# Four experts and a channel attention joined in one block, three quarters normalised ahead, TensorE's fillers and the value matrix moved

## The chip, the cores and the metric

One core of one Trainium2 chip runs the whole program in one launch. The metric is the device time of one execution in microseconds (us). Engines are named as in the profile: PE (TensorE matmul), PEld (its weight loads), DVE (VectorE), ACT (ScalarE), POOL (GpSimd), SP (SyncE).

## The reference, cut to what matters

A tower of four layers on 4 x 512 tokens of width 64, in float32. The residual stream is `h`; every half layer is `h = h + f(layernorm(h))`. The change touches the second half of L1, all of L2, and the way into L3:

```python
h = h + _L1_attn_ref(_layernorm(h, axis=-1), ...)    # softmax attention, one head
h = h + _L1_ffn_ref(_layernorm(h, axis=-1), ...)     # graph scores, then 4 experts, top 2
h = h + _L2_attn_ref(_layernorm(h, axis=-1), ...)    # channel attention
h = h + _L2_ffn_ref(_layernorm(h, axis=-1), ...)     # 8 experts, top 2
h = h + _L3_attn_ref(_layernorm(h, axis=-1), ...)    # softmax attention, 8 heads
h = h + _L3_ffn_ref(_layernorm(h, axis=-1), ...)     # causal attention, then 8 experts
# channel attention, per batch and per head of 4 channels:
k, v = layernorm(k), layernorm(v)                    # over groups of 4 channels, ddof 1, gain, offset
kv = einsum('bhnd,bhne->bhde', k, v) / HW
out = einsum('bhnd,bhde->bhne', q, kv)
return gelu((out + x) @ W_proj.T + b_proj) + x
```

## The kernel before, in words

The 2048 tokens are 16 tiles of 128. A quarter q (0 to 3) is the 4 tiles of one batch, 512 tokens. `H` holds the residual stream, `X` the normalised input, both tokens by channels; `XT2` is `X` turned, channels by tokens. PSUM has 8 banks, `PS[:, bank]`. Each engine's order is written out by hand and held together by semaphores; a `Block` ends with a barrier of all engines.

**experts** (line 1432; 4 experts in L1, 8 in L2, there as 4 pairs) walks over 16 units (quarter, expert): PE `up` (L1473), ACT the activation (L1542), PE `gates` (L1484) spreads the gate weights, DVE multiplies (L1570), PE `down` (L1504). At a quarter's end ACT copies one output bank (L1548), DVE adds the other (L1576), PE turns the sum back (`turn`, L1511), and DVE adds it to `H` in two steps (L1561, L1563). With an `Entering` object in `after`, the next stage's layernorm of quarters 0 to 2 runs meanwhile: DVE `sums` (L2240, L2242), POOL `centre` (L2250, L2253), DVE `root` (L2259, L2261), POOL `apply` (L2268, L2271). A quarter's `sums` and the previous one's `root` stand in DVE's order between its other work. With `keeps_turn`, the turn of the last quarter is left to the next stage as `before["last_turn"]`.

**L1's experts** (`l1_ffn`, L3208) have none of this: the block ends, and **l2_attn** (L3271) opens a block whose `entry` normalises all four quarters on DVE and ACT (L2342 to L2352), turns them on PE (L2533) and copies them on ACT (L2510), while POOL prepares the weights (`kv_weights`, 18 small chained steps, L3249) and then adds `X` to `H` for all tiles in one instruction (L3421).

**The channel attention** projects keys and values (`kv`, L3300) and queries (L3306) and the skip path (`skip`, L3315). Each quarter goes through five DVE steps, in `schedule`, skewed by two: step 0 adds the bias out of PSUM (L3441), ACT squares (L3393), step 1 sums (L3445), ACT roots (L3398), step 2 adds epsilon (L3448), step 3 is the reciprocal (L3451), step 4 the product (L3454). I write (k,q) for step k of quarter q. Gain and offset are two POOL instructions per quarter (L3425, L3427), for the last quarter two DVE instructions (L3477, L3480). Then per quarter: PE `met` (L3322), DVE `masked_` (L3458), PE `mixing` (L3331), ACT copies (L3402), PE `heads` (L3341), DVE adds the bias (`biased`, L3464), ACT applies gelu (L3406), POOL adds to `H` (L3430), DVE for the last one (L3468).

**unread** (L3346, L368, L851) and **dense** (L2546) are matmuls whose result nobody reads; they only fill TensorE's time.

**l2_ffn** (L3491) has its `entry`, the experts with `after`, and in the same block **l3_attn**, which is `linked_attentions` (L643). At its start PE turns the value matrix (L754) and quarter 0 (L2293), does the kept turn, projects (L765), and runs the 8 row products `rows` (L775), whose maxima DVE takes (L1000); DVE splits them in five steps (`split`, L1011 to L1019), PE turns them (`maxima`, L797), and the columns and exponentials follow (L807, L816, L941). The value matrix `VO` is cleared, given its ones and filled by DVE at this stage's start (L976, L978, L983); row products wait for it because it frees a bank. Eight `unread` stand ahead of `maxima(0)`.

**l1_attn** is `softmax_attention` (L189), with 4 `unread` ahead of its row products (L303), 2 after each of the four, and 6 later; POOL meanwhile normalises the last quarter twice (L2250 to L2280), and that quarter's turn (L2293) stands ahead of `maxima(0)` (L317).

## Time and profile before

| what | us |
|---|---|
| runs, median of 3 | 918.92 (918.06 to 924.89) |
| the profiled execution, its own time | 922.85 |
| its span, first to last instruction | 921.0 |
| PE busy | 808.4 (88%) |
| DVE busy | 644.0 (70%) |
| ACT busy | 370.6 (40%) |
| POOL busy | 231.7 (25%) |
| mean granted clock of PE | 0.947 |

The times in all rows are us from the span's start. The clock is a share of full speed: 1.00 is 2.4 GHz, 0.50 is 1.2 GHz. DMA plays no part in the stages at issue.

### The profile page before, as it was taken

Reading aid. Unit: us, or ns where it says so; the run is one execution under the profiler, and the core shown is the slowest. Engines: PE = TensorE matmul, PEld = TensorE weight load, DVE = VectorE, ACT = ScalarE, POOL = GpSimd, SP = SyncE. Lnnn points to the kernel's source line nnn. Section 1 sums busy time; section 2 is a strip of 40 time slices with the busy share of each in tenths; the row PEclk is TensorE's granted clock in tenths of the full one; section 3 lists DMA queues with packets and bytes.
Section 4 is the critical chain, followed back from the end, with each engine's and each line's share of the span. In section 5 each row is a group of like instructions: output and inputs, shape, how many; then the busy total and the mean of one; then the engine's idle time right before and its main releaser. Section 6 shows DMA issues by size and latency. Waiting matters only on the chain. (4 is left out here: it accounts for less than half of the span.)

```text
span 921.0 us, 19874 instructions
## 1 busy us (share of the span) xinstructions
PE 808.4 (88%) x8099; PEld 432.8 (47%) x8099; DVE 644.0 (70%) x1724; ACT 370.6 (40%) x642; POOL 231.7 (25%) x292
## 2 busy tenths in 40 slices
PE   0896879979999887998788979999999999978997
PEld 0566757755544345774365433333333334434443
DVE  3988548877896468998775874656566456757665
ACT  0213354444663342323544614555554333344443
POOL 1900003223546213440150131113132424210000
PEclk9898989998999999999986978999999998997999
DMA  8500030000000001000000000000000000000000
GB/s 284 159 1 2 1 96 3 3 2 2 1 1 2 1 2 49 1 2 1 1 2 1 1 1 1 1 1 1 2 1 2 1 1 1 2 1 1 7 7 13
DMA packets 11494, 15.28 MB, mean 17 GB/s; under 512 B 8390, under 2 KB 9446, under 8 KB 10406
## 3 DMA queue, kind: packets, MB, share of 16 engines
q1 hardware_dynamic: 9984, 12.91, 4.5%
q10 hardware_dynamic: 1418, 1.09, 0.5%
q8 instruction: 65, 1.06, 0.5%
q14 instruction: 27, 0.22, 0.1%
HBM read 13.47 MB, written 0.52 MB: 15 GB/s over the span
## 5 line engine op out<-in xcount | busy, mean ns | idle before, releaser
L1000 DVE TENSOR_REDUCE mx<-PS 128x2 f32<-128x1024 f32 (+3 forms) x96 | 102.4, 1088 | 71.1 <-PE PS L775 59.4
L941 ACT ACTIVATE arena<-PS 128x1024 f32<-128x1024 f32 (+3 forms) x96 | 85.8, 917 | 122.2 <-PE PS L816 109.0
L807 PE MATMUL PS<-arena 32*128 32x512 f32 (+3 forms) x384 | 90.8, 611 | 7.4 <-ACT arena L927 2.7
L775 PE MATMUL PS<-arena 32*128 32x512 f32 (+3 forms) x384 | 90.6, 640 | 4.4 <-DVE arena L983 3.8
L832 PE MATMUL PS<-arena 128*64 128x512 f32 (+3 forms) x384 | 92.3, 565 | 0.4 <-DVE arena L1059 0.4
L1542 ACT ACTIVATE arena<-PS,f_b_sb 128x512 f32<-128x512 f32 x96 | 61.2, 684 | 38.5 <-PE PS L1473 35.0
L1570 DVE TENSOR_TENSOR arena<-arena,PS 128x512 f32<-128x512 f32 x96 | 61.6, 683 | 15.5 <-PE PS L1484 15.5
L1473 PE MATMUL PS<-XT,late 64*64 64x512 f32 x384 | 61.5, 606 | 2.9 <-issue 1.5
L1504 PE MATMUL PS<-arena,late 64*64 64x512 f32 x384 | 58.1, 596 | 0.0
L1104 POOL TENSOR_TENSOR H<-H,arena 128x256 f32<-128x256 f32 x32 | 23.5, 736 | 116.9 <-DVE arena L1034 114.5
L807 PEld LDWEIGHTS PS<-arena 32*128 32x128 f32 x384 | 27.6, 189 | 53.0 <-issue 32.2
L1754 DVE TENSOR_TENSOR arena<-arena,PS 106x512 f32<-106x512 f32 (+1 forms) x48 | 30.8, 684 | 20.9 <-PE PS L1654 13.7
L2546 PE MATMUL PS<-identh 128*128 128x512 bf16 x91 | 29.5, 464 | 16.8 <-PEq L1197 4.0
L2072 PE MATMUL PS<-late 128*128 128x128 fp8e5 x512 | 35.6, 235 | 8.3 <-DVE late L1981 8.3
L832 PEld LDWEIGHTS PS<-arena 128*64 128x64 f32 x384 | 19.9, 136 | 46.7 <-issue 39.9
L1722 ACT ACTIVATE arena<-PS 106x512 f32<-106x512 f32 (+1 forms) x48 | 26.0, 594 | 39.2 <-PE PS L1642 39.2
L775 PEld LDWEIGHTS PS<-arena 32*128 32x128 f32 x384 | 28.3, 198 | 25.4 <-issue 14.9
L2072 PEld LDWEIGHTS PS<-late 128*128 128x128 fp8e5 x512 | 32.9, 106 | 13.0 <-DVE late L1981 11.0
L3047 POOL TENSOR_TENSOR arena<-NB,vals 128x1280 f32<-128x1280 bf16 x11 | 25.7, 2339 | 35.2 <-DVE vals L3122 35.2
L1395 POOL TENSOR_TENSOR H<-H,arena 128x256 f32<-128x256 f32 x28 | 20.4, 730 | 53.0 <-DVE arena L1358 50.9
L1059 DVE SCALAR_TENSOR_TENSOR arena<-arena,Cc 128x256 f32<-128x256 f32 x32 | 15.6, 498 | 25.4 <-ACT arena L941 25.2
L1642 PE MATMUL PS<-XT,late 64*64 64x512 f32 (+1 forms) x192 | 30.8, 612 | 1.0 <-DVE L L2368 1.0
(480 smaller groups left out, 1724.0 us busy)
## 6 DMA issues: line engine op xcount, KB each, us to landing
arena<-in_rel SPq DMA_DIRECT2D x4, 1024.0 KB, 11.8
late<-in_edges SPq DMA_DIRECT2D x2, 1024.0 KB, 11.7
arena<-in_adj SPq DMA_DIRECT2D x1, 1024.0 KB, 6.6
late<-in_w_f_w SPq DMA_DIRECT2D x2, 512.0 KB, 3.9
Cc<-in_consts SPq DMA_DIRECT2D x1, 916.0 KB
arena<-in_ids ACTq DMA_DIRECT2D x1, 800.0 KB
late<-in_w_f_w SPq DMA_DIRECT2D x2, 340.0 KB, 3.7
late<-in_w_f_w SPq DMA_DIRECT2D x4, 128.0 KB, 2.8
```

The source lines that it names most:

```text
L775: ins = nc.tensor.matmul(PS[:, a + j, keys(g, c)], QT[h, g % 3, c * P:(c + 1) * P], KT[h, g % 3, keys(g, c)], start=True, stop=not late(g) ...
L807: ins = nc.tensor.matmul(PS[:, a + j, queries(g, c)], KT[h, g % 3, c * P:(c + 1) * P], QT[h, g % 3, queries(g, c)], start=not less_first, ...
L832: ins = nc.tensor.matmul(PS[half(j), 6 + p, queries(g, c)], XO[:, batch(g) * TB + c, :], PT[:, s % 2, p, j, queries(g, c)], start=c == 0, ...
L941: nc.scalar.activation(PT[:, s % 2, p, :, queries(g, c)], PS[:, a:a + 2, queries(g, c)], ACT.Exp, scale=of(g).scale).then_inc(exp_done.sem, 1)
L1000: v.reduce_max(mx[:, g % 2, c, 2 * p:2 * p + 2], PS[:, a:a + 2, keys(g, c)], axis=AX.X).then_inc(max_done.sem, 1)
L1473: ins = nc.tensor.matmul(PS[half(m), up_bank(n), :], w1(i)[r, half(m)], XT2[r, b * S:(b + 1) * S], start=True, stop=True, skip_group_check ...
L1504: ins = nc.tensor.matmul(PS[half(i), banks[m], :], w2(i)[half(m)], HG[half(m), n % 4, :], start=m == 1 and i < 2, stop=i >= T - 2, skip_gr ...
L1542: nc.scalar.activation(HA[:, n % 3, :], PS[:, up_bank(n), :], act_fn, bias=b1(tiles[n][1])).then_inc(hidden_done.sem, 1)
L1570: v.tensor_tensor(HG[:, n % 4, :], HA[:, n % 3, :], PS[:, gate_bank(n), :], ALU.mult).then_inc(gated_done.sem, 1)
L1642: ins = nc.tensor.matmul(PS[m, z, :], w1(*tile)[half(z), m], XT2[half(z), b * S:(b + 1) * S], start=True, stop=True, skip_group_check=True)
L1754: nc.vector.tensor_tensor(HG[0:rows_of(r), n % 4, :], HA[0:rows_of(r), n % 3, :], PS[0:rows_of(r), 2 + z, :], ALU.mult).then_inc(gated_don ...
L2072: ins = nc.tensor.matmul(PS[:, 6 + m % 2, n * P:(n + 1) * P], spelt[k % 3][:, g, P:2 * P], spelt[k % 3][:, g, 0:P], start=g % GROUP == 0, ...
```

## The change

It does five things. (1) L1's experts take an `Entering`, keep their last turn and share a block with `l2_attn`; the `entry` between them is gone. Quarters 0 to 2 are normalised during the experts by DVE and POOL, quarter 3 inside the channel attention by the same two. `kv_weights` runs on POOL beside the experts, into another part of the arena. (2) PSUM banks and PE's order in the channel attention are dealt anew; the add of `X` to `H` moves on POOL from ahead of the gains to behind quarter 0's. (3) The tail: `masked_(1)` goes ahead of (4,3), all masks one place earlier, more `unread` (17 from `met(0)` on, in place of 5; 6 ahead of it). (4) `VO` is made on DVE during the 8 experts (at unit 8, and its copy late in the experts); in `linked_attentions` 4 `unread` go behind the projection, one behind each of the 8 row products, and the 8 ahead of `maxima(0)` go. (5) In `softmax_attention` the 8 `unread` between row products go.

```diff
@@ softmax_attention, tensor
                 for s in range(TB):
                     rows(s)
-                    unread(2, a=7)
@@ linked_attentions, tensor
                 proj(0)
+                unread(4, a=7)
                 for s in range(TB):
-                    rows(s)
+                    for p in range(NPAIR):
+                        row_products(s, p)
+                        unread(1, a=7)
                 proj(1)
                 eng.wait_ge(out_added.sem, before["out_added"])
-                unread(8)
                 maxima(0)
@@ linked_attentions, vector
-                v.memset(VO[:], 0.0).then_inc(vo_ready.sem, 1)
-                eng.wait_ge(vo_ready.sem, at(vo_ready, 0))
-                v.tensor_scalar(VO[:, :, D:D + 1].rearrange("p a b -> p (a b)"), C["last"].to_broadcast([P, 4]), 1.0, None, ALU.mult).then_inc(vo_ready.sem, 1)
...
-                values_turned(first, bank(("V", 0, 0)), 0)
@@ l1_ffn
-                    ACT.Gelu, one_gate, H, H, b1=lambda e: w("f1_b1")[:, e:e + 1], b2=b2h[:, 1], block=block, entered=then)
+                    ACT.Gelu, one_gate, H, H, b1=lambda e: w("f1_b1")[:, e:e + 1], b2=b2h[:, 1], aside=kv_weights, block=block, entered=then, after=after, keeps_turn=True)
+            l2_attn(after, block, then)
@@ l2_attn, tensor
-                for q in range(B - 1):
-                    kv(q)
-                for q in range(B):
-                    queries(q)
+                for q in range(2):
+                    entered.turn(eng, q, turn_bank(q))
+                before["last_turn"]()
+                kv(0)
+                entered.turn(eng, 2, turn_bank(2))
+                kv(1)
+                queries(0)
+                queries(1)
+                kv(2)
+                unread(8, MIXING)
+                entered.turn(eng, B - 1, turn_bank(B - 1))
+                skip(0)
+                queries(2)
+                queries(3)
                 kv(B - 1)
-                skip(0)
...
+                skip(1)
+                eng.wait_ge(kv_steps[B - 1].sem, 1)
+                skip(2)
+                skip(B - 1)
+                eng.wait_ge(q_out.sem, 1)
+                for k, q in schedule[schedule.index((0, B - 1)) + 1:schedule.index(MET_AT)]:
                     eng.wait_ge(kv_steps[q].sem, k + 1)
...
+                    unread(2)
+                k, q = MET_AT
+                eng.wait_ge(kv_steps[q].sem, k + 1)
+                met(0)
+                eng.wait_ge(q_out.sem, 2)
+                unread(4, MIXING)
+                mixing(0)
+                met(1)
+                heads(0)
                 mixing(1)
-                unread(2)
+                unread(4)
                 met(2)
                 heads(1)
                 mixing(2)
-                unread(1)
+                unread(3)
                 met(3)
                 heads(2)
                 mixing(3)
-                unread(1)
+                unread(2)
                 heads(3)
@@ l2_attn, scalar
+                for q in range(B - 1):
+                    entered.turned_out(eng, q, turn_bank(q))
...
-                        if q in (1, 2):
-                            q_copy(q - 1)
+                        if q == 1:
+                            q_copy(0)
+                        if q == 2:
+                            entered.turned_out(eng, B - 1, turn_bank(B - 1))
+                        if q == B - 1:
+                            q_copy(1)
@@ l2_attn, gpsimd
-                for q in range(B):
-                    eng.wait_ge(norm_steps[q].sem, normed[q])
-                nc.gpsimd.tensor_tensor(H[:], H[:], X[:], ALU.add).then_inc(skip_added.sem, 1)
+                entered.centre(eng, B - 1, 0)
+                entered.apply(eng, B - 1, 0)
+                entered.normed(eng, B - 1)
                 for q in range(B - 1):
...
+                    if q == 0:
+                        nc.gpsimd.tensor_tensor(H[:], H[:], X[:], ALU.add).then_inc(skip_added.sem, 1)
@@ l2_attn, vector
+                entered.sums(eng, B - 1, 0)
                 for k, q in schedule:
                     step(k, q)
+                    if (k, q) == (2, 0):
+                        entered.root(eng, B - 1, 0)
                     if (k, q) == MASK_AT:
                         masked_(0)
+                    if (k, q) == NEXT_MASK_AT:
+                        masked_(1)
@@ l2_ffn
+        def values_begun(eng, n):
+            if n == 8:
...
+        def values_turned(eng):
+            eng.wait_ge(vo_turned.sem, turned + 1)
+            nc.vector.tensor_copy(VO[:, :, 0:D], PS[:, 0, 0:4 * D].rearrange("p (n d) -> p n d", d=D)).then_inc(vo_ready.sem, 1)
```

## Rows read from the trace of the kernel before

**Rows 1.** The page: busy time of each engine, and the clock in 40 slices
```profile
PE 808.4 (88%) x8099; PEld 432.8 (47%) x8099; DVE 644.0 (70%) x1724; ACT 370.6 (40%) x642; POOL 231.7 (25%) x292
...
PEclk9898989998999999999986978999999998997999
```

**Rows 2.** Windows: stretch, length, busy us of PE, PEld, DVE, ACT, POOL, clock
```profile
475.00:480.00 5.00, 3.25 (x31) 1.93 (x30) 5.00 (x8) 2.43 (x4) 3.53 (x4) 1.00 0.00 0
...
485.00:490.00 5.00, 5.00 (x39) 3.98 (x40) 0.86 (x3) 0.53 (x2) 1.16 (x2) 0.50 0.00 0
490.00:495.00 5.00, 3.23 (x17) 1.69 (x18) 2.54 (x7) 2.23 (x5) 0.73 (x1) 0.50 0.00 2
...
545.00:550.00 5.00, 5.00 (x18) 1.86 (x16) 5.00 (x5) 0.00 (x0) 0.00 (x0) 0.50 0.00 0
```

**Rows 3.** Timeline of the join: start, length, engine, line, instruction
```profile
451.56 1.09 PE L1504 MATMUL PS<-arena,late 64*64 64x512 f32 x8
...
455.26 0.42 DVE L1563 TENSOR_TENSOR H<-PS,H 128x256 f32<-128x256 f32 x1
...
463.38 2.36 POOL L3421 TENSOR_TENSOR H<-H,X 128x1024 f32<-128x1024 f32 x1 [0.42 <-POOL arena L3269]
...
466.74 0.69 DVE L3441 TENSOR_TENSOR arena<-PS,arena 128x512 f32<-128x512 f32 x1 [4.48 <-PE PS L3300]
```

**Rows 4.** Timeline of the 8 experts' end, where the next layernorm runs beside
```profile
531.43 1.09 PE L1504 MATMUL PS<-arena,late 64*64 64x512 f32 x8
...
534.53 0.61 POOL L2271 TENSOR_TENSOR X<-tA,st 128x256 f32<-128x256 f32 x1
...
537.67 0.42 DVE L1563 TENSOR_TENSOR H<-PS,H 128x256 f32<-128x256 f32 x1
...
538.49 0.61 POOL L2271 TENSOR_TENSOR X<-tA,st 128x256 f32<-128x256 f32 x1
```

**Rows 5.** Timeline of the channel attention's steps, then two groups of them
```profile
474.36 1.27 POOL L3427 TENSOR_TENSOR arena<-arena 128x512 f32<-128x512 f32 x1
...
474.91 0.81 DVE L3448 TENSOR_SCALAR chan<-chan 128x128 f32<-128x128 f32 x1
...
477.27 1.28 ACT L3399 ACT_TABLE_LOAD   x1
...
480.58 0.86 DVE L3454 TENSOR_TENSOR arena<-arena,chan 128x512 f32<-128x512 f32 x1
...
L3451 DVE RECIPROCAL chan<-chan 128x128 f32<-128x128 f32 x4 | 3.8, 939 | 0.0
...
L3425 POOL TENSOR_TENSOR arena<-arena 128x512 f32<-128x512 f32 x3 | 3.8, 1268 | 8.7 <-DVE arena L3454 8.7
```

**Rows 6.** Timeline of the same products at full and at half clock; last instruction
```profile
477.82 0.68 PE L3322 MATMUL PS<-arena 128*64 128x64 f32 x8 [0.25 <-DVE chan L3451]
...
487.80 1.12 PE L3322 MATMUL PS<-arena 128*64 128x64 f32 x8
...
492.99 0.43 DVE L3468 TENSOR_TENSOR H<-H,Y 128x256 f32<-128x256 f32 x1 [0.55 <-ACT Y L3406]
```

**Rows 7.** Timeline of the linked attentions' start
```profile
538.72 1.43 DVE L978 TENSOR_SCALAR arena<-Cc 128x4 f32<-128x4 f32 x1
...
540.33 10.00 PE L775 MATMUL PS<-arena 32*128 32x512 f32 x32 [3.82 <-DVE arena L983]
...
542.44 9.16 DVE L1000 TENSOR_REDUCE mx<-PS 128x2 f32<-128x1024 f32 x8 [2.28 <-PE PS L775]
...
552.27 2.30 PE L851 MATMUL PS<-identh 128*128 128x512 bf16 x8
...
554.41 0.39 PE L797 MATMUL PS<-identh,arena 128*128 128x128 bf16 x4
```

**Rows 8.** Timeline of L1's attention, before its first columns
```profile
302.68 0.61 POOL L2271 TENSOR_TENSOR X<-tA,st 128x256 f32<-128x256 f32 x1
...
303.44 1.09 PE L2293 MATMUL PS<-Cc,X 128*64 128x128 f32 x16 [0.86 <-POOL X L2271]
```

More of the change, by code:

```diff
@@ L3278, in l2_attn @@
         MET, MIXING = 6, 7
-        kv_bank = lambda q: 2 * (q % (B - 1))
-        head_bank = lambda q: (2, 4, 0, 0)[q]
+        kv_bank = lambda q: (2, 4, 0, 2)[q]
+        head_bank = lambda q: (4, 0, 2, 4)[q]
+        turn_bank = lambda q: (0, 1, 0, MIXING)[q]
         head_at = lambda q, c: (q == B - 1) * P + c * D
         tiles_of = lambda q, r: [q * TB + 2 * c + r for c in range(2)]
-        with nc.Block() as block:
-            entry([Norm(H, X)], turned=XT2[:], aside=kv_weights, block=block)
-            turned = turned_copied.count - B
-            normed = [norm_steps[q].count for q in range(B)]
+        entered.received()
+        with nullcontext():
             @block.tensor
@@ L3342, in heads, with unread @@
                     ins.then_inc(heads_mixed.sem, 1)
-                def unread(n):
+                def unread(n, a=MET):
                     for _ in range(n):
-                        nc.tensor.matmul(PS[:, MET, :], identh[:], bc(identh[:], 1, TB), start=True, stop=True, skip_group_check=True)
-                for q in range(B - 1):
-                    kv(q)
-                for q in range(B):
-                    queries(q)
-                kv(B - 1)
-                skip(0)
-                for k, q in schedule[schedule.index((2, 0)):]:
-                    if k == 0:
-                        skip(q - 1)
-                        if q == B - 1:
-                            skip(q)
-                        continue
-                    if (k, q) == (2, 0):
-                        eng.wait_ge(q_out.sem, 1)
-                    eng.wait_ge(kv_steps[q].sem, k + 1)
-                    if (k, q) == MET_AT:
-                        met(0)
-                    elif (k, q) == MIX_AT:
-                        mixing(0)
-                        unread(1)
-                        met(1)
-                        heads(0)
-                    elif schedule.index((k, q)) < schedule.index(MET_AT):
-                        unread(2)
@@ L3380, in _ @@
                 mixing(3)
-                unread(1)
+                unread(2)
                 heads(3)
@@ L3481, in _ @@
                 biased(0)
-                masked_(2)
+                masked_(3)
                 biased(1)
-                masked_(3)
                 biased(2)
@@ L3495, in l2_ffn @@
             experts(8, 4, lambda g: w("f2_w1")[:, g // 2 * P:(g // 2 + 1) * P], lambda g: w("f2_w2")[:, g * D:(g + 1) * D],
-                    ACT.Gelu, lambda g, m: picked(2 * g + m, D), H, H, b1=lambda g: w("f2_b1")[:, g:g + 1], b2=b2h[:, 2], block=block, entered=then, after=after, keeps_turn=True)
+                    ACT.Gelu, lambda g, m: picked(2 * g + m, D), H, H, b1=lambda g: w("f2_b1")[:, g:g + 1], b2=b2h[:, 2], block=block, entered=then, after=after, keeps_turn=True, between=values_begun, values=values_turned)
             l3_attn(after, to_causal, block, then)
```

36 lines of the change are left out of this document (22 added, 14 removed).

## The prediction

> **What bounds the kernel now.** I read the page first. PE is busy 88% of the span and its clock dips in the middle [rows 1], so no engine's share says what this change is worth: it touches four short stretches, and each has its own last wait. I took the timeline of each stretch, then windows for the clock. Three things are to be seen.
>
> First, the join of the 4 experts and the channel attention. Count from the end of the experts' last `down`, 452.65 = 451.56 + 1.09, as zero. The last quarter is in `H` at 3.0, and DVE's first channel step starts only at 14.1 (466.74) [rows 3]. The 11 us between are a barrier and a layernorm, turn and projection of all quarters with nothing beside them. The DVE chain then runs to 28.8 (481.44) [rows 5] and a tail to 40.8 (493.42) [rows 6].
>
> Second, that tail. The clock is 1.00 up to 480, 0.50 from 485 to 495 [rows 2]. The same eight `met` records take 0.68 at full and 1.12 at half clock [rows 6].
>
> Third, the linked attentions' start. Row products wait 3.82 us for the value matrix (L983), which stood behind a small DVE instruction of 1.43; then everything runs at half clock, DVE's 8 maxima take 9.16, and `maxima(0)` starts at 554.41 although the maxima were finished at 551.60, because 8 fillers at 2.30 stand ahead [rows 2, 7].
>
> **Part 1, the join (quarters 0 to 2 normalised early).** The trace has this arrangement at the end of the 8 experts, so I take times from there, zero being 532.52: `X` of quarter 1 ready at 2.6, `H` of the last quarter at 5.6, `X` of quarter 2 at 6.6 [rows 4]. So the last quarter comes 2.5 later than now, and the first step earlier. PE turns quarter 1 (1.09 each [rows 8]), does the kept turn and kv(0) until 5.4. DVE, busy with `H` and the last quarter's sums, does (0,0) at 6.8 to 7.5, against 14.1: 7.3 ahead.
>
> That lead shrinks. ACT has the copy of turned quarter 2 ahead of its first square; PE's turn waits for the `X` of 6.6, so the copy ends at 8.6 and (1,0) is done at 10.1. The load of the root's table, 1.28 for any such load [rows 5], was done beforehand by the removed `entry` and now stands between square and root: (2,0) at 11.1. The last quarter's `root` follows to 12.0, POOL's `apply` to 13.9 (1.9), turn and copy to 15.9, two queries and kv(3) to 17.7, (0,3) to 18.5.
>
> Here POOL matters. In the rows a short DVE instruction (L3448, normally 0.2) that started during a POOL instruction took 0.81 and ended just behind it, at 475.72 against 475.63 [rows 5]: DVE stood until POOL was through. In the changed order POOL gets quarter 0 at 15.3, is through gain and offset (2 x 1.27 [rows 5]) at 18.0, then adds `X` to `H`, 2.36 [rows 3], until 20.4. (2,2), due at 18.5, falls into it and waits 1.9. (4,1) ends at 21.3, POOL's quarter 1 lasts to 24.1, (2,3) waits for it, (4,2) ends at 25.0. POOL's quarter 2 lasts to 27.7, and (4,3), held up by `masked_(1)` and POOL, ends at 28.3. That is only 0.5 ahead of now's 28.8. Bounds: if no DVE step met the long add, 26.0; if POOL's instructions and DVE's fell worst throughout, another 1.3 (one POOL instruction), 29.6. I take 28.3, as the row at 474.91 shows the hold.
>
> The Trainium skill's page "SBUF — State Buffer", section "Who interferes with whom", says that a DVE instruction with two SBUF inputs or in a two-port mode and a reading GpSimd one exclude each other for the whole instruction. By that, the 2.36 us add blocks as written; no run here yet shows a hold so long. By an even sharing instead, the stage would end about 2 us earlier.
>
> What hides the rest: `kv_weights` on POOL ends some 4 us before POOL's first `centre`, beside the experts, whose pace is PE's; if it didn't, `X` of quarter 0 would be late by as much. The layernorms' DVE instructions lie in DVE's gaps there; I charge 0.1, bounds 0 and 0.5. The 8 `unread` on bank 7 lie in the wait for the last quarter's `X`. The removed wait of skip and queries costs nothing: both are ready.
>
> **Part 2, the tail.** Now it takes 12.0 from (4,3) to the end, at half clock. After, from 28.3: DVE gain to 29.0, `masked_(2)` 29.2, offset 29.9; `met(3)` 0.68 and its wait 30.9; mask 31.2, mixing and copy 32.0, heads 32.7, then bias, gelu and sum 0.42 + 0.42 + 0.43 [rows 6] and gaps: 34.2. The 17 fillers (0.22 each at full clock: 2.30 for 8 at mostly half clock is 0.29 [rows 7], so about two thirds of it) lie in waits for DVE and POOL if the clock stays full. If it doesn't, they are on the chain; I work that out with the rivals. Parts 1 and 2: 40.8 - 34.2 - 0.1 = **6.5 less**; bounds 0 (half clock) and 8.8 (no hold by the long add).
>
> The next `entry` starts at half clock now [rows 2], and its first turn is a little late behind fillers: **0.3 less**, bounds 0 and 0.6.
>
> **Part 3, the linked attentions.** The value matrix's three DVE instructions move into the experts. The copy fits a wait of DVE for POOL ahead of `root`, the other two the gaps at unit 8: 0. Row products then wait for the queries' copies, at 537.7 instead of 540.33; four fillers end before. At full clock the first maximum starts at 538.9 against 542.44: 3.5 less. DVE's 1.145 per maximum stays the pace, as a product plus one filler is about as short (an estimate: eight such records take 1.09 at full clock [rows 3], and their drain lies under the filler's 0.22). So the last maximum ends at 548.1, the split at 549.2. `proj(1)` is done by then, no fillers stand ahead, `maxima(0)` at 549.4 against 554.41: 5.0 less. PE idles 2.4 us before it, so I allow 0.8 for a dip there: **4.2 less**, bounds 5.2 less and 2.8 more (below).
>
> **Part 4, L1's attention.** Eight fillers go. The turn of the last quarter waits for POOL's `X` at 303.29 and starts at 303.44 [rows 8]; row products end long before either way. So nothing is gained: the fillers lay beside POOL's chain. PE's wait before that turn grows from 0.86 to 2.8, which may cost clock behind it: **0.6 more**, bounds 0 and 1.7 (half clock for 3.4 us over turn, projection and first columns).
>
> **Sum**, against the profiled execution's 922.85 (span 921.0 and 1.85 around it): -6.5 - 0.3 - 4.2 + 0.6 = -10.4, so 912.4. That execution lies 3.9 above the median of 918.92, inside the spread of the runs shown. I carry the difference over: 918.9 - 10.4 = **908.5**. Some of the 3.9 may be the very dips that go; that is a reason for the range to reach up.
>
> **Rivals.** *A, the slower one: the clock stays at half in both places, and the fillers are on the chain.* What decides is whether PE is active enough before `met(0)` and in the row products. For it: the clock fell at about 481 after a stretch with 3.25 of 5 busy, and the small products never brought it back, though PE counts as busy all the time [rows 2]; in the new order PE waits about 2 us for the long POOL add. Price: from `masked_(1)` on, at half clock, fillers 9 x 0.43, `met` and heads 1.1 each, mixing 0.5 give an end at about 40.6, so nothing gained in the join; row products can't overlap across a filler that uses the whole array, 8 x 2 x 1.09 = 17 us against 9.16, less the fillers that went, 2.8 more; L1's attention 1.5 more: 918.9 + 4.3 - 0.3 = **923**. Against it: fillers more than triple, and their wait at 540 is gone.
>
> *B, the tail alone at half clock*, row products at full: 918.9 - 0 - 4.2 + 0.6 = **915**.
>
> *C, the long add misses DVE's instructions*: (2,2) is issued ahead of POOL's add, or one of two sources is read unhindered. Then 2.3 more is won: **906**; with full clock throughout and nothing lost in L1's attention **904**.
>
> *D, the join wins nothing because H's last quarter comes 2.5 us later and every quarter waits for POOL's slower layernorm.* For it: the lead of 7.3 at (0,0) is down to 0.5 at (4,3) in my own sum. It is the same as my forecast in part 1 and would need 1.5 us more of POOL: **910**.
>
> **Chances.** Forecast 0.45, C 0.17, D 0.15, B 0.15, A 0.08. The time is that of the forecast, 908.5; the range 903.5 to 916.5 holds C, D and B and leaves out A and a better C. A measurement of this kernel tells about 1% (9.2 us) from no change, so faster means below 909.7: most of the forecast's case, C, and a little of D: 0.55. Within 1%: 0.42. Slower by over 1%, above 928: 0.03, beyond even A as priced.
>
> **What would show it.** Right: the first L3441 7 us after the last `down`, not 14; an ACT table load between the first L3393 and the first L3398; a DVE step of about 2 us ending with POOL's 2.4 us add; the stage's end 34 us after the last `down`; clock 1.00 in the tail; the 8 maxima starting some 6.4 us after the last `down`, `maxima(0)` at 16.9 where it is 21.9 now. Wrong: half clock in tail or row products; (4,3) before 27 or behind 30; the turn of the last quarter in L1's attention earlier than now, which would mean the fillers had been on the path.

## The result, and the profile after

The changed kernel takes 915.84 us in the median of 11 runs (913.90 to 922.22), the kernel before 922.32 in 11 runs beside them (918.06 to 926.89): ratio 0.9931, 95% interval 0.9912 to 0.9950. So it is faster, by 6.5 us from median to median, where I had forecast 10.4. The other part of the distance between 908.5 and 915.84 is the foot: the median of 918.92 that I subtracted from rested on three runs, and with eight more, eleven in all, it is 922.32. The profiled execution of the changed kernel is its slowest, 922.22 us with a span of 920.1, against before's span of 921.0. A difference of 0.9 between two traces while the medians differ by 6.5 is itself a lesson of this case; the section on the stretches side by side shows what it is made of.

The page of the changed kernel, to be read beside [rows 1]: POOL has 12 us more (the layernorms of the channel attention), DVE 4 less, and the clock's row has another pattern.

```profile
PE 813.2 (88%) x8086; PEld 437.3 (48%) x8086; DVE 640.0 (70%) x1720; ACT 367.2 (40%) x633; POOL 243.6 (26%) x308
...
PEclk9886989998999996999798998999999999997999
```

**The join.** Timeline of the changed kernel (start, length, engine, line, instruction), the lines that answer to [rows 3, 5, 6]. Zero is again the end of the last `down`, 462.14 + 1.09 = 463.23.

```profile
462.14 1.09 PE L1500 MATMUL PS<-arena,late 64*64 64x512 f32 x8
...
468.39 0.42 DVE L1559 TENSOR_TENSOR H<-PS,H 128x256 f32<-128x256 f32 x1
...
469.75 0.68 DVE L3454 TENSOR_TENSOR arena<-PS,arena 128x512 f32<-128x512 f32 x1
...
472.63 1.28 ACT L3409 ACT_TABLE_LOAD   x1
472.65 0.69 DVE L3458 TENSOR_REDUCE chan<-arena 128x128 f32<-128x512 f32 x1 [2.21 <-ACT arena L3400]
...
480.42 0.69 DVE L3454 TENSOR_TENSOR arena<-PS,arena 128x512 f32<-128x512 f32 x1 [1.16 <-PE PS L3294]
480.47 2.35 POOL L3440 TENSOR_TENSOR H<-H,X 128x1024 f32<-128x1024 f32 x1
481.03 1.87 DVE L3461 TENSOR_SCALAR chan<-chan 128x128 f32<-128x128 f32 x1
...
483.42 0.67 DVE L3458 TENSOR_REDUCE chan<-arena 128x128 f32<-128x512 f32 x1
483.58 1.27 POOL L3436 TENSOR_TENSOR arena<-arena 128x512 f32<-128x512 f32 x1 [0.76 <-DVE arena L3467]
484.02 0.94 DVE L3464 RECIPROCAL chan<-chan 128x128 f32<-128x128 f32 x1
...
484.88 0.16 DVE L3461 TENSOR_SCALAR chan<-chan 128x128 f32<-128x128 f32 x1
484.92 1.26 POOL L3438 TENSOR_TENSOR arena<-arena 128x512 f32<-128x512 f32 x1
484.99 1.75 DVE L3467 TENSOR_TENSOR arena<-arena,chan 128x512 f32<-128x512 f32 x1
485.12 1.12 PE L3320 MATMUL PS<-arena 128*64 128x64 f32 x8
...
488.69 0.22 DVE L3471 TENSOR_TENSOR KVm<-PS,Cc 64x64 f32<-64x64 f32 x1 [0.97 <-PE PS L3320]
488.83 1.13 DVE L3467 TENSOR_TENSOR arena<-arena,chan 128x512 f32<-128x512 f32 x1
...
496.67 0.43 DVE L3481 TENSOR_TENSOR H<-H,Y 128x256 f32<-128x256 f32 x1 [0.92 <-ACT Y L3417]
```

Read it from the top: (0,0) starts at t = 6.5 (before 14.1), (1,0) is done at 10.1, the last quarter's (0,3) ends at 17.9, and (2,2), an instruction of 0.2 us, takes 1.87 and ends as POOL's add of 2.35 ends. (2,3), 0.16 long, slips in between POOL's gain and offset of quarter 1 (the two POOL rows at 483.58 and 484.92), and then (4,2) is held by the offset and takes 1.75. Between (2,2) and (4,2) the reduce and the reciprocal have their normal lengths although POOL works beside them: not every DVE instruction is held. (4,3) ends at t = 26.7 and the stage at 33.9, against 28.8 and 40.8 before.

Windows of the changed kernel (columns as in [rows 2]), over the tail of the channel attention, then the row products of the linked attentions:

```profile
475.00:480.00 5.00, 4.71 (x46) 2.78 (x46) 4.26 (x8) 2.06 (x5) 3.66 (x4) 1.00 0.00 0
480.00:485.00 5.00, 3.83 (x38) 1.99 (x34) 4.58 (x7) 2.06 (x4) 4.16 (x4) 0.90 0.00 0
485.00:490.00 5.00, 5.00 (x40) 3.12 (x40) 4.00 (x6) 1.37 (x4) 3.71 (x3) 0.76 0.01 3
490.00:495.00 5.00, 5.00 (x54) 3.22 (x53) 2.81 (x7) 1.43 (x5) 0.92 (x2) 1.00 0.00 0
...
545.00:550.00 5.00, 5.00 (x22) 1.36 (x18) 4.38 (x5) 0.00 (x0) 0.54 (x3) 1.00 0.00 0
```

The tail runs at 0.76 to 1.00 where it ran at 0.50 from 485 on, and the row products at 1.00 where they ran at 0.50. The 0.76 is a dip around `met(0)`, whose eight records at 485.12 take 1.12 as at half clock; DVE waits 0.97 for PE in front of `masked_(1)`, the row at 488.69, before it comes to (4,3).

**The linked attentions**, timeline of the changed kernel, against [rows 7]. The last `down` of the 8 experts ends at 535.39 + 1.09 = 536.48.

```profile
542.82 1.23 DVE L996 TENSOR_REDUCE mx<-PS 128x2 f32<-128x1024 f32 x1 [0.76 <-PE PS L774]
543.02 1.13 PE L774 MATMUL PS<-arena 32*128 32x512 f32 x4
...
544.08 0.39 PE L850 MATMUL PS<-identh 128*128 128x512 bf16 x1
544.20 1.23 DVE L996 TENSOR_REDUCE mx<-PS 128x2 f32<-128x1024 f32 x1 [0.15 <-PE PS L774]
544.40 1.13 PE L774 MATMUL PS<-arena 32*128 32x512 f32 x4
...
555.00 0.38 PE L796 MATMUL PS<-identh,arena 128*128 128x128 bf16 x4 [1.19 <-DVE arena L1015]
```

The first maximum starts 6.3 after the last `down`, and `maxima(0)` 18.5 after it (before 21.9). But the maxima start 1.38 apart, not 1.145: DVE waits 0.15 in front of each, and between two products of 1.13 on PE stands a filler.

**L1's attention**, windows of the kernel before and, in the second fence, of the changed one:

```profile
300.00:310.00 10.00, 8.66 (x79) 4.20 (x82) 4.05 (x10) 3.76 (x6) 4.04 (x12) 1.00 0.00 0
340.00:360.00 20.00, 15.67 (x185) 11.93 (x181) 16.33 (x52) 7.12 (x15) 5.24 (x6) 0.91 0.17 57
```

```profile
300.00:310.00 10.00, 6.33 (x50) 3.64 (x48) 5.00 (x12) 1.71 (x3) 5.89 (x14) 0.83 0.00 0
...
340.00:360.00 20.00, 16.78 (x128) 12.50 (x127) 13.93 (x47) 7.55 (x17) 4.36 (x7) 0.60 0.01 2
```

And the turn of the last quarter in the changed kernel, which waits for POOL's `X` as in [rows 8] but now has idled 3.48 before it and runs slower (1.73 where 1.09 stood):

```profile
305.42 0.61 POOL L2267 TENSOR_TENSOR X<-tA,st 128x256 f32<-128x256 f32 x1
306.17 1.73 PE L2289 MATMUL PS<-Cc,X 128*64 128x128 f32 x16 [3.48 <-POOL X L2267]
```

### The profile page after: what moved, and what is told of

The parts are those of the page before. It is cut to its first block and busy times, and to the rows that moved or that the text cites. A ratio compares the mean times of both kernels' runs of the same rounds, so it can differ in the third digit from the quotient of the medians.

```text
span 920.1 us, 19832 instructions
## 1 busy us (share of the span) xinstructions
PE 813.2 (88%) x8086; PEld 437.3 (48%) x8086; DVE 640.0 (70%) x1720; ACT 367.2 (40%) x633; POOL 243.6 (26%) x308
## 3 DMA queue, kind: packets, MB, share of 16 engines
q10 hardware_dynamic: 1418, 1.09, 0.5%
## 5 line engine op out<-in xcount | busy, mean ns | idle before, releaser
L806 PE MATMUL PS<-arena 32*128 32x512 f32 (+3 forms) x384 | 89.3, 591 | 7.4 <-ACT arena L928 2.7
L774 PE MATMUL PS<-arena 32*128 32x512 f32 (+3 forms) x384 | 88.8, 590 | 0.8 <-DVE mx L996 0.4
L1538 ACT ACTIVATE arena<-PS,f_b_sb 128x512 f32<-128x512 f32 x96 | 61.1, 684 | 40.4 <-PE PS L1469 36.9
L1469 PE MATMUL PS<-XT,late 64*64 64x512 f32 x384 | 63.4, 623 | 2.9 <-issue 1.5
L1100 POOL TENSOR_TENSOR H<-H,arena 128x256 f32<-128x256 f32 x32 | 23.5, 734 | 117.2 <-DVE arena L1030 114.8
L806 PEld LDWEIGHTS PS<-arena 32*128 32x128 f32 x384 | 27.3, 184 | 53.9 <-issue 32.8
L1750 DVE TENSOR_TENSOR arena<-arena,PS 106x512 f32<-106x512 f32 (+1 forms) x48 | 30.8, 684 | 20.9 <-PE PS L1650 13.7
L2068 PE MATMUL PS<-late 128*128 128x128 fp8e5 x512 | 37.9, 242 | 7.0 <-DVE late L1977 7.0
L2068 PEld LDWEIGHTS PS<-late 128*128 128x128 fp8e5 x512 | 34.9, 110 | 12.0 <-DVE late L1977 8.2
L2542 PE MATMUL PS<-identh 128*128 128x512 bf16 x80 | 27.4, 487 | 14.7 <-PEq L1193 4.0
L2264 POOL TENSOR_TENSOR st<-st,Cc 128x4 f32<-128x4 f32 x24 | 24.4, 1018 | 42.1 <-DVE st L2257 42.1
L774 PEld LDWEIGHTS PS<-arena 32*128 32x128 f32 x384 | 26.6, 184 | 18.7 <-issue 10.9
L1055 DVE SCALAR_TENSOR_TENSOR arena<-arena,Cc 128x256 f32<-128x256 f32 x32 | 15.5, 495 | 23.7 <-ACT arena L942 23.5
```

The costliest lines, as they stand in the source:

```text
L774: ins = nc.tensor.matmul(PS[:, a + j, keys(g, c)], QT[h, g % 3, c * P:(c + 1) * P], KT[h, g % 3, keys(g, c)], start=True, stop=not late(g) ...
L806: ins = nc.tensor.matmul(PS[:, a + j, queries(g, c)], KT[h, g % 3, c * P:(c + 1) * P], QT[h, g % 3, queries(g, c)], start=not less_first, ...
L1469: ins = nc.tensor.matmul(PS[half(m), up_bank(n), :], w1(i)[r, half(m)], XT2[r, b * S:(b + 1) * S], start=True, stop=True, skip_group_check ...
L1538: nc.scalar.activation(HA[:, n % 3, :], PS[:, up_bank(n), :], act_fn, bias=b1(tiles[n][1])).then_inc(hidden_done.sem, 1)
L1750: nc.vector.tensor_tensor(HG[0:rows_of(r), n % 4, :], HA[0:rows_of(r), n % 3, :], PS[0:rows_of(r), 2 + z, :], ALU.mult).then_inc(gated_don ...
L2068: ins = nc.tensor.matmul(PS[:, 6 + m % 2, n * P:(n + 1) * P], spelt[k % 3][:, g, P:2 * P], spelt[k % 3][:, g, 0:P], start=g % GROUP == 0, ...
```

## The experiments

Fifteen experiments, in four groups; three of them run a kernel a second time. The runs of before beside them have medians of 922.0 to 924.3. A kernel's executions spread over 7 to 15 us, so a difference of one or two microseconds between two medians is not resolved here; some stretches of the trace are, since they repeat to 0.1 or 0.2 from trace to trace; the table at the end shows which do and which don't. I read both, the stretch first.

### Which part is worth what

**The changed kernel again**, and the parts undone one at a time.

> The changed kernel once more, unaltered, as the foot for the three runs beside it. Theory 1 (parts add, the loss is upstream chance): a ratio of 0.993 again, and a profile whose stretch from the last down of the 4 experts to the end of the channel stage is 33.9 us again, whatever the clock in 340-360 us does. Theory 2 (the change itself brings the half clock at the entry of the graph, by its shorter L1 attention): the clock in 340-360 us is 0.6 again and the start of the graph late by 4 us against the kernel before.

916.79 us (12 runs), ratio 0.9921 (0.9896 to 0.9947). Same result. Its profiled execution is 916.21, and the clock in 340 to 360 is 0.79. The graph starts 32.0 behind L1's attention, against 34.9 in the first trace and 30.2 before, so theory 2's 0.6 and 4 us are not fixed to this kernel, and a loss of 1.8 is left. In this trace `met(0)` runs at full clock, (4,3) ends 25.4 behind the last `down` (26.7 in the first trace), and the stage ends at 33.3 (33.9).

```diff
                 for s in range(TB):
                     rows(s)
+                    unread(2, a=7)
```

> Part 4 alone undone: the eight fillers between the row products of L1's attention are back, all else as changed. Theory 1 (they only held the clock behind the turn): 0.6 to 1.3 us faster than the changed kernel. Theory 2 (without them the clock stays low through the attention's start and the next entries, which is why 10.4 us of gain came out as 6.4): 4 us faster than the changed kernel, ratio to before 0.989. Rival (they cost nothing and hid nothing): the same within 0.3 us.

915.21 us (6 runs), 0.9907 (0.9874 to 0.9940). The windows of this kernel, beside the two fences above:

```profile
300.00:310.00 10.00, 8.97 (x84) 3.89 (x88) 3.55 (x6) 4.19 (x6) 2.18 (x9) 1.00 0.01 2
340.00:360.00 20.00, 14.89 (x165) 11.10 (x165) 16.42 (x49) 6.62 (x14) 6.01 (x6) 0.91 0.17 57
```

Both are back at before's clock. The same kernel, in more runs:

> The kernel with the eight fillers of L1's attention back once more, because its median rested on few runs. Theory (read off ten profiles: all eight kernels without these fillers show a clock of 0.83 in 300 to 310 us, and seven of the eight then need 31.9 to 35.0 us from the attention's end to the graph, where with them it is 30.1): 1.3 us won before the first columns and about 2 between the attention and the graph, so 3 us faster than the changed kernel in the median, ratio to before 0.989 to 0.991. Rival (the second loss is chance): 1.3 us faster, ratio 0.9915.

914.23 us (12 runs), 0.9914 (0.9883 to 0.9945): 0.7 to 1.7 parts in a thousand below the changed kernel, and 0.9914 is the rival's 0.9915 (fillers worth 1.3 us); the interval also holds the theory's 0.989 to 0.991, so a second loss behind the attention is not shown by the times.

```diff
-                unread(4, a=7)
                 for s in range(TB):
-                    for p in range(NPAIR):
-                        row_products(s, p)
-                        unread(1, a=7)
+                    rows(s)
                 proj(1)
                 eng.wait_ge(out_added.sem, before["out_added"])
+                unread(8)
                 maxima(0)
...
                 v = nc.vector
+                v.memset(VO[:], 0.0).then_inc(vo_ready.sem, 1)
+                eng.wait_ge(vo_ready.sem, at(vo_ready, 0))
...
+                values_turned(first, bank(("V", 0, 0)), 0)
```

> Part 3 alone undone: value matrix, row products and fillers of the linked attentions as before; join, tail and L1's attention as changed. Theory 1 (as the profile pair reads): 3.4 to 5.0 us slower than the changed kernel, ratio to before 0.997 to 0.999. Rival (the gain at maxima is given back inside the linked attentions): slower by under 1.5 us.

917.83 us (10 runs), 0.9936 (0.9915 to 0.9957): 0.5 to 1.5 parts in a thousand above the changed kernel, the rival's size. The intervals overlap. In its trace `maxima(0)` comes 1.8 later after the last `down` than in the changed kernel, not 3.4: with the join in place, the old arrangement of part 3 was no longer as slow as in the kernel before (clock 0.76 in 540 to 550 where it was 0.50).

> Parts 1 and 2 alone undone: the kernel before with part 3 and part 4 of the change. Theory 1 (parts add): faster than before by 2.1 to 3.7 us (3.4 to 5.0 of the linked attentions less 1.3 of L1's attention), ratio 0.996 to 0.998; 6 to 7 us slower than the changed kernel. Rival (the join and tail win less in most executions than in the profiled pair, because the clock dips elsewhere in the tail): only 2 to 3 us slower than the changed kernel.

Before, with parts 3 and 4 only: 925.76 us (12 runs), 1.0020 (0.9992 to 1.0048), so not faster than before at all and 9 us above the changed kernel. Locally it has what it should (+1.3 in L1's attention, -3.4 at `maxima(0)`). The next kernel is the one before with part 3 alone:

> The kernel before with part 3 of the change alone (value matrix early, four fillers ahead of and one behind each row product of the linked attentions). Theory 1 (local sums carry over): maxima(0) 19.1 us behind the last down of the 8 experts instead of 22.5, 3.4 us faster than before, ratio 0.996. Theory 2 (part 3 pays its gain back in later clock dips, read off the kernel with parts 3 and 4 and without the join, 3 us slower than before where 2 us faster was due): the same 3.4 us at maxima(0), but a clock of 0.5 to 0.8 somewhere in 740 to 800 us and a ratio of 0.998 to 1.003.

921.58 us (12 runs), 0.9983 (0.9956 to 1.0009). The ratio lies in theory 2's range, and its interval reaches theory 1's 0.996 too. The dip that theory 2 asks for is there (clock 0.66 in 760 to 780), but the second trace of before has one as deep (0.66 in 780 to 800), so it is nothing that part 3 brings. This kernel and the previous one differ in L1's eight fillers alone, and by 3.7 parts in a thousand, 3.4 us: more than the 1.3 that the fillers are worth in their own stretch, though the two intervals overlap and the two traces don't say where the rest would lie (attention's end to the graph: 31.7 with the fillers, 29.9 without).

> The kernel before, unaltered, for a second trace of it. Theory (the spread is where clock dips fall): between the end of L1's attention and the graph 30 us, from the last down of the 4 experts to the stage's end 41.3, and maxima(0) 22.5 behind the last down of the 8 experts, each within 0.3; the dips behind 700 us elsewhere than in the first trace. Rival (these stretches vary by themselves): a change of over 1 us in one of the three, which would take its share from the change.

924.11 us, one run. The three stretches came out at 30.2, 41.3 and 22.5: the local sums start from numbers that repeat in this kernel. With part 3 in and the join not, the same old stage takes 39.7.

### What sets the pace of the maxima

```diff
                     for p in range(NPAIR):
                         row_products(s, p)
-                        unread(1, a=7)
```

> The changed kernel without the one filler behind each row product of the linked attentions (the four ahead of them stay, the value matrix stays early). My step in the prediction said that the maxima keep DVE's pace of 1.145 us with or without the filler. Theory 1 (the filler is in the loop: a bank comes free, product, filler, next product): without it the maxima are 1.145 apart instead of 1.38 and maxima(0) starts 17.3 us behind the last down of the 8 experts instead of 19.1. Rival (the fillers buy the clock): the maxima are 1.145 apart, but the clock is at 0.5 behind them, the first columns are slow, and the whole is 1 to 3 us slower.

917.02 us (11 runs), 0.9942 (0.9914 to 0.9971). Theory 1 is right, and of the rival the clock. The timeline gives the eight maxima 9.15 us, 1.144 each, and `maxima(0)` comes 1.7 earlier:

```profile
534.04 9.15 DVE L995 TENSOR_REDUCE mx<-PS 128x2 f32<-128x1024 f32 x8 [0.76 <-PE PS L774]
```

and the windows show what that costs:

```profile
535.00:540.00 5.00, 4.67 (x18) 1.76 (x18) 5.00 (x6) 0.00 (x0) 1.64 (x8) 0.76 0.00 0
540.00:545.00 5.00, 4.44 (x14) 1.20 (x12) 4.64 (x10) 1.02 (x2) 0.08 (x1) 0.50 0.00 0
545.00:550.00 5.00, 4.97 (x19) 1.90 (x20) 2.74 (x4) 1.92 (x3) 1.15 (x2) 0.50 0.00 0
```

Half clock from 540 on, although PE counts as busy 4.4 to 5.0 of 5 us. The rest of the linked attentions takes 269.2 in this trace, the longest of all traces. In the median the kernel is 1 to 2 parts in a thousand above the changed one, and the intervals overlap: that the eight fillers win more behind the maxima than the 1.7 they cost ahead is not shown by the times. The 1.7 also says that what part 3 wins up to `maxima(0)` comes from the early value matrix and the eight fillers that went, not from the clock.

```diff
-                        unread(1, a=7)
+                        nc.tensor.matmul(PS[:, 7, 0:2 * P], identh[:], bc(identh[:], 1, 2), start=True, stop=True, skip_group_check=True)
```

> The changed kernel with the filler behind each row product of the linked attentions at 256 columns instead of 512. Theory 1 (product plus filler set the pace of 1.38 us, and a filler of any length keeps the clock): the maxima are 1.145 to 1.2 apart, maxima(0) starts 17.4 to 17.8 us behind the last down instead of 19.1, and the clock stays at 1.00 behind them, where the kernel without these fillers fell to 0.50. Rival (the clock asks for the full filler): the pace is the same, but the clock is at 0.50 in the ten microseconds around the end of the maxima.

914.87 us (11 runs), 0.9931 (0.9893 to 0.9968). The eight maxima take 10.13, 1.27 each, and `maxima(0)` comes 0.7 earlier than in the changed kernel; the clock stays at 1.00 until 545, past `maxima(0)` at 543.5, and is 0.82 in 545 to 550 and 0.50 in 550 to 555. The changed kernel dips behind its maxima as well (0.75 in 560 to 565, 0.57 in 565 to 570, `maxima(0)` at 555.0). Half the filler's length gives back about half of what it costs, and keeps the clock until the maxima are done.

### POOL's long add, the table, the tail

```diff
-                    if q == 0:
+                    if q == B - 2:
                         nc.gpsimd.tensor_tensor(H[:], H[:], X[:], ALU.add).then_inc(skip_added.sem, 1)
```

> The changed kernel with POOL's add of X to all of H moved from behind quarter 0's affine to behind quarter 2's. Theory 1 (a POOL instruction with two inputs in SBUF holds DVE out until its end): the step (2,2) takes 0.2 to 0.4 us instead of 1.87, the last (4,3) ends about 25 us behind the last down instead of 26.7, and the hold comes back in the tail, where DVE's gain of the last quarter or its offset now takes up to 2.4 us; the stage is 1 us shorter to 1 us longer. Rival (the long step was something else): (2,2) stays long, and no step of the tail becomes long.

918.97 us (11 runs), 0.9958 (0.9926 to 0.9990), 2 to 3 us above the changed kernel in the median with overlapping intervals, though its stage is 0.5 to 1.1 shorter in the trace. Theory 1 holds for the hold. DVE's steps in this kernel:

```profile
480.66 0.22 DVE L3462 TENSOR_SCALAR chan<-chan 128x128 f32<-128x128 f32 x1
480.79 0.68 DVE L3468 TENSOR_TENSOR arena<-arena,chan 128x512 f32<-128x512 f32 x1
...
488.75 2.39 DVE L3499 TENSOR_TENSOR arena<-arena 128x512 f32<-128x512 f32 x1
```

(2,2) takes 0.22, and the hold has moved to the last quarter's offset: 2.39 instead of 0.67, under POOL's add at 487.80. (4,3) ends 23.9 behind the last `down`. Whose turn it is to wait can be chosen.

```diff
                 entered.centre(eng, B - 1, 0)
+                for q in range(B - 1):
+                    entered.normed(eng, q)
+                rest = slice(0, (B - 1) * TB)
+                nc.gpsimd.tensor_tensor(H[:, rest], H[:, rest], X[:, rest], ALU.add).then_inc(skip_added.sem, 1)
                 entered.apply(eng, B - 1, 0)
                 entered.normed(eng, B - 1)
+                rest = quarter(B - 1)
+                nc.gpsimd.tensor_tensor(H[:, rest], H[:, rest], X[:, rest], ALU.add).then_inc(skip_added.sem, 1)
...
-                    if q == 0:
-                        nc.gpsimd.tensor_tensor(H[:], H[:], X[:], ALU.add).then_inc(skip_added.sem, 1)
```

> The changed kernel with POOL's long add cut in two and moved: X is added to H's quarters 0 to 2 behind the centre of the last quarter, where POOL waits for 3.9 us, and to the last quarter behind its apply. Theory 1 (the hold by a POOL instruction with two inputs costs what stands on DVE's chain): (2,2) takes 0.22 us instead of 1.87, no step of the tail becomes long, and the stage is 1.4 to 1.9 us shorter than the changed kernel's 33.8 to 34.5 (from the start of the last down). Rival (the three-quarter add of about 1.8 us now holds up (1,0) and with it the last quarter's root): under 0.5 us shorter.

915.10 us (12 runs), 0.9930 (0.9897 to 0.9963). The stage is 31.8 from the start of the last `down`, 2.1 under the changed kernel's second trace and 2.7 under its first: more than forecast. POOL's two adds in this kernel:

```profile
463.40 1.82 POOL L3434 TENSOR_TENSOR H<-H,X 128x768 f32<-128x768 f32 x1
468.62 0.73 POOL L3438 TENSOR_TENSOR H<-H,X 128x256 f32<-128x256 f32 x1
```

The large one fills POOL's wait and a pause of DVE, the small one holds one step to 0.77, and nothing of the tail is held by an add. In the median of the whole kernel 2 us don't stand out.

```diff
                 for q in range(B - 1):
+                    if q == B - 2:
+                        nc.scalar.activation(idle[:, 0:1], C["eps"][:, 0:1], ACT.Sqrt).then_inc(table_set.sem, 1)
                     entered.turned_out(eng, q, turn_bank(q))
```

> The changed kernel with one more idle Sqrt activation on ACT, ahead of the copy of turned quarter 2, so that the root's table is loaded before the first square. Theory 1 (the load of 1.28 us stands on the chain square, root, (2,0)): (2,0) and with it the root, apply, turn and kv(3) of the last quarter come 1.0 to 1.3 us earlier, and the stage ends 0.5 to 1.2 us earlier. Rival (the hold by POOL's long add takes it up): (2,2) is blocked longer, until the same end of POOL's add, and the stage ends within 0.3 us of now.

915.71 us (11 runs), 0.9932 (0.9901 to 0.9963); the stage is 0.3 shorter, as the rival says, but not for its reason. Much of the load lay beside DVE's reduce (0.69) and the step behind it, as the fence of the join shows (472.63 and 472.65), so (2,0) came only 0.5 earlier. (2,2) is not held longer, as the rival has it, but 1.77 instead of 1.87.

```diff
                 met(0)
                 eng.wait_ge(q_out.sem, 2)
-                unread(4, MIXING)
                 mixing(0)
...
-                unread(4)
+                unread(2)
...
-                unread(3)
+                unread(1)
...
-                unread(2)
+                unread(1)
```

> The changed kernel with the fillers of the channel attention's tail as few as before: none ahead of mixing(0), then 2, 1 and 1 instead of 4, 3 and 2. Theory 1 (the fillers hold the clock): the granted clock behind met(0) falls to 0.5, met takes 1.12 instead of 0.68, and from the end of (4,3) to the end of the stage it takes 9 to 12 us instead of 7.1. Rival (the tail is short because of its new order, and the fillers stand in waits): 6.5 to 7.1 us, clock as now.

917.83 us (11 runs), 0.9957 (0.9926 to 0.9988). Windows of its tail:

```profile
475.00:480.00 5.00, 3.29 (x36) 2.14 (x34) 4.75 (x8) 1.89 (x4) 4.22 (x4) 1.00 0.01 3
480.00:485.00 5.00, 4.53 (x33) 3.63 (x35) 2.44 (x6) 0.53 (x2) 1.14 (x2) 0.52 0.00 0
485.00:490.00 5.00, 2.86 (x22) 1.96 (x21) 1.67 (x5) 1.47 (x5) 1.41 (x2) 0.50 0.01 2
```

Half clock again, and a stage of 35.9 instead of 33.8. So the nine fillers taken out here (of the 13 from `met(0)` on) are worth 2 us. The rest of the tail's gain is its new order: at half clock it takes 10.2 from the end of (4,3), the old one 12.0.

### Together

> The changed kernel with three edits together: the eight fillers of L1's attention back, POOL's add of X to H early and in two, and the root's table loaded early. If the parts add: 1.3 to 3 from the fillers, 1.4 to 1.9 from the add and 0.3 from the table, so 3 to 5 us faster than the changed kernel, ratio to before 0.987 to 0.990. Rival (what is won in one stretch is lost to clock dips in a later one, as the spread of the runs suggests): within 1 us of the changed kernel.

909.44 us (6 runs, 906.85 to 918.78), 0.9881 (0.9828 to 0.9933): the L1 fillers, the early adds and the early table make the fastest kernel of the case, 1.2% under before and some 6 us under the changed kernel, though with six runs the two intervals still overlap a little. In the trace the stage is 31.4, L1's attention needs 13.2, and the way to the graph 30.3.

> The kernel with three edits (L1's fillers back, POOL's add early and in two, root's table early) and the 256-column fillers behind the row products. If the parts add: another 0.7 us at maxima(0) (18.4 instead of 19.1 behind the last down of the 8 experts), ratio to before 0.987. Rival (the shorter filler costs clock behind the maxima): within 0.5 us of the kernel with three edits or slower.

911.70 us (6 runs), 0.9884 (0.9844 to 0.9924). With the short product fillers on top `maxima(0)` comes at 18.4 from the start of the last `down`, as expected, and in the median that is nothing, as the rival has it.

### The stretches side by side

Each number is the distance in us between two starts in one profiled execution, good to 0.1: a, first row product to first column of L1's attention; b, last filler behind that attention to the first gather of the graph; c, graph's last to the 4 experts' last `down`; d, that `down` to the stage's end (the end of the last add to `H`); e, on to the 8 experts' last `down`; f, on to `maxima(0)`; g, on to the last mix of the linked attentions. The change edits a, d and f; it also puts layernorms and `kv_weights` beside the 4 experts in c, and the value matrix's instructions beside the 8 experts in e.

| kernel | a | b | c | d | e | f | g |
|---|---|---|---|---|---|---|---|
| before | 13.2 | 30.2 | 35.7 | 41.3 | 38.5 | 22.5 | 265.2 |
| before, second trace | 13.2 | 30.2 | 35.6 | 41.4 | 38.5 | 22.5 | 268.8 |
| part 3 alone | 13.2 | 31.7 | 37.0 | 39.6 | 40.1 | 19.1 | 267.2 |
| parts 3 and 4 | 14.5 | 29.9 | 36.8 | 39.7 | 38.5 | 19.1 | 268.7 |
| changed | 14.4 | 34.9 | 37.4 | 34.5 | 38.8 | 19.1 | 263.7 |
| changed, second trace | 14.4 | 32.0 | 37.2 | 33.8 | 38.6 | 19.1 | 264.8 |
| part 3 undone | 14.4 | 31.9 | 37.2 | 33.9 | 38.6 | 20.9 | 265.7 |
| L1 fillers back | 13.2 | 30.1 | 37.2 | 34.6 | 40.3 | 19.1 | 268.4 |
| L1 fillers back, second trace | 13.2 | 30.4 | 35.5 | 33.4 | 40.4 | 19.1 | 264.8 |
| three edits | 13.2 | 30.3 | 35.5 | 31.4 | 39.6 | 19.1 | 267.5 |

What the reader is to see: a and f repeat to 0.1 and follow their edits exactly. b and g, which no edit touches, take values that lie 5 to 6 us apart, c and e such that lie 2 apart, and the opening, before a, ends anywhere between 290 and 299 us. Where windows were read, the longer value goes with a further dip of the clock (b: 0.60 in 340 to 360 for 34.9, 0.91 for 30.2). What lies beside the 4 experts is not what makes c long: the two kernels without the join have 36.8 and 37.0 as well, and five with it 35.5 to 35.7; the long ones start the experts with a longer time at low clock (0.62, 0.50 and 0.86 in the three windows of 5 us from 435 on in the changed kernel, one window of 0.66 in the kernel before). And what L1's fillers win in b comes back in part in e, which is 39.6 to 40.4 in the four traces of changed kernels that have these fillers, and 39.1 on average in the nine that don't. In the pair of traces that I compared first, b alone gives back 4.7 and c 1.7 of the 8.9 won in a, d and f, and the opening another 2.7.

## Why the prediction was right and wrong

**Direction and mechanism: right.** All four parts act where I placed them. **Size: too large**, 10.4 against 6.5. The steps that failed are these terms of the sum: the maxima's pace, taken as 1.145 and measured at 1.38 (part 3 brought 3.4 and not 4.2); L1's attention, taken as 0.6 and measured at 1.3; the next entry, taken as 0.3 and measured at 0; and the stretches that the diff doesn't edit, put at nothing without a reason, where the first trace of the changed kernel lost 4.7 (b), 1.7 (c) and 2.7 (the opening). That 915.84 lies inside the range, and beside rival B's 915, is luck: the foot was 3.4 too low, and B's half clock in the tail did not come. By the prediction's own steps:

*The join and the tail, -6.5.* Measured -6.9 in the pair, 33.9 against the 34.2 forecast and 40.8 before; over all traces 5 to 8, since the old stage takes 39.6 to 41.4 from the start of that `down` and the new one 33.4 to 34.6. The path as far as (2,2) was right down to the instruction: (0,0) at 6.5 (forecast 6.8), (1,0) at 10.1 (10.1), table load between square and root, (2,2) held 1.7 by the long add (1.9). (0,3) came 0.6 and (4,3) 1.6 before my figures: (2,3) did not wait for POOL's quarter 1 as I had it, and (4,2) ended at 23.5 instead of 25.0. (4,3) before 27 was on my own list of signs of being wrong, and it is so in both traces (26.7 and 25.4); the path between (2,2) and (4,3) was worked out too long. The tail took 7.1 and not 5.9: DVE waits for PE 0.43 and 1.07 in front of the last two masks and 0.97 in front of the last bias, behind products and fillers that I had made shorter. (In the second trace it is 7.9, with POOL holding the gain for 1.64.) So the stage's end at 33.9 for 34.2 is two errors, of 1.6 and 1.2, that cancel. The fillers from `met(0)` on are 4, 4, 3 and 2, so 13 and not the 17 that I counted; five became thirteen, which is not "more than triple". By the Trainium skill, page "SBUF — State Buffer", section "Who interferes with whom", the hold lasts for the whole GpSimd instruction and a reduce is never held on this chip; the trace and the runs with the add moved agree on both (1.87 against 0.22, and reduces of 0.67 to 0.69 beside POOL). That disposes of rival C, that the add misses DVE, and of the 2 us by even sharing. Rival B, the tail at half clock, is what the run with few tail fillers shows, at 2 us and not at the 6.5 I gave it. Rival D is wrong: the join wins. Its own price of 910 allowed for 1.5 us less gain only, not for none.

*The next entry, -0.3.* Measured 0: from the stage's end to the first `up` of the 8 experts it is 12.9 in both kernels.

*The linked attentions, -4.2.* Measured -3.4. The clock came back, the first maximum was where I put it (6.3 for 6.4), and there is no dip in front of `maxima(0)`, for which I had allowed 0.8. The step that failed is "DVE's 1.145 per maximum stays the pace, as a product plus one filler is about as short". The product's records take 1.13 and the filler adds 0.25: 1.38, over seven gaps 1.6 us, and `maxima(0)` at 18.5 for 16.9. I had let the products' drain lie under the filler; the rows from 543.02 to 544.40 show product, filler and next product in turn, with 0.07 of overlap between records. Without the filler the pace is 1.144 and the clock is gone.

*L1's attention, +0.6.* Measured 1.3, twice my figure. In its own stretch it is that in every one of the ten traces without the fillers, inside my bounds. But I let its cost end at the first columns. Behind it, from that attention's end to the graph, the traces without the fillers need 29.8 to 34.9 (ten of them, mean 32.1), those with them 30.0 to 31.7 (seven, mean 30.4), so another 1.7 on average, of which the 8 experts' stretch gives some back; and the two kernels that differ in these fillers alone lie 3.4 us apart where part 3 is the rest of the change, 1 to 2 where all of it is, with overlapping intervals both times. The 1.3 is shown; that the whole cost is more, perhaps above my upper bound of 1.7, is likely by the traces and not shown by the times.

*The sum.* I counted every stretch that the diff doesn't edit at zero. The medians say that 8.9 to 9.5 of local gain became 6.5. Up to 1.7 of the difference may be the stretch just named. The rest lies within the scatter of c, e and g over single traces, and these runs don't settle where: the cause of this part stays open.

*The foot.* 918.92 was low by 3.4, and my remark that the profiled execution lay 3.9 above the median had it the wrong way round: 922.85 was the ordinary time.

## What to carry to other kernels

Fillers that wait beside another engine's chain are not free to take away because they are off the path: here taking away eight of them, worth nothing by the chain, cost 1.3 us of low clock behind a turn. In a loop over banks a filler is one of the loop's terms, so add its length to the product's before saying which engine sets the pace, and try a shorter one while the trace still shows the clock held. Where spread between executions is larger than the gain, build the sum from stretches that repeat, check which of the others don't, and put the latter's spread into the range; and before adding an elementwise instruction to POOL look for a pause that POOL and DVE have in common.

## What the runs showed that I had not expected

The half clock comes with PE counted busy: 4.44 and 4.97 of 5 us in the two windows from 540 to 550 without the product fillers, 5.00 of 5 in the kernel before [rows 2]. Eight fillers of 256 columns, one behind each product, kept 1.00 until the maxima were done.

A hold between DVE and POOL falls on single kinds of instruction. Beside POOL's two-input work a tensor_scalar of 0.22 took 1.87 and a multiply of 0.68 took 1.75, a reduce kept 0.67 and a reciprocal 0.94. POOL is held in turn: in the run with the add last, its add beside the held DVE steps took 2.79. And the hold can be moved: the same 2.35 us add held a step in the middle, the last offset (2.39), or, in two parts where DVE paused, nothing that mattered.

Dips of the clock fall in different stretches, edited or not, from execution to execution: the span of one and the same kernel, the changed one, went from 908.7 to 920.1, and the first profile of each kernel, 921.0 and 920.1, would have called this change worthless.
